# Weighted rows stored slot by slot within a feature, and half-chunks of gathers left out, in the two GAT layers of a four-layer graph network

## The reference

```python
def gat_conv(h, src, dst, fc_w, attn_l, attn_r, bias, heads, out_feats):
    feat = (h @ fc_w.T).reshape(n, heads, out_feats)
    el = jnp.sum(feat * attn_l, axis=-1)
    er = jnp.sum(feat * attn_r, axis=-1)
    e = jax.nn.leaky_relu(el[src] + er[dst], 0.2)
    m = jax.ops.segment_max(e, dst, num_segments=n)
    ex = jnp.exp(e - m[dst])
    ssum = jax.ops.segment_sum(ex, dst, num_segments=n)
    a = ex / ssum[dst]
    rst = jax.ops.segment_sum(feat[src] * a[..., None], dst, num_segments=n)
    return rst + bias.reshape(heads, out_feats)
...
h0 = gat_conv(inputs, src, dst, fc1_w, attn_l1, attn_r1, bias1, 8, 32)
h1 = jax.nn.relu(h0 + norm * (inputs @ wb0.T + bb0))
h2 = gat_conv(h1, src, dst, fc2_w, attn_l2, attn_r2, bias2, 1, 256)
```

## Time and profile before

| what | value |
|---|---|
| median of 3 runs | 7953.76 us (7950.26 to 7963.52) |
| the profiled execution, its own time | 7953.61 us |
| its span in the trace | 7951.9 us |
| busy in the span | DVE 70%, POOL 67%, PE 42%, ACT 16% |
| gat1, roughly from 3260 to 4540 us | 1280 us |
| gat2, roughly from 4540 to 5830 us | 1290 us |

### The profile page before, as it was taken

One profiled execution on the slowest core, in us unless ns is written; L12 is line 12 of the kernel. 1 busy time (PEld: TensorE's weight loads), 2 busy tenths in 40 slices (PEclk: granted clock), 3 DMA queues, 4 the chain that ended last, 5 costly groups with the idle time before them and its releaser, 6 DMA issues. The chain is left out here.

```text
span 7951.9 us, 73782 instructions
## 1 busy us (share of the span) xinstructions
PE 3326.4 (42%) x15180; PEld 2659.3 (33%) x15181; DVE 5588.3 (70%) x11215; ACT 1251.3 (16%) x2729; POOL 5351.3 (67%) x4985
## 2 busy tenths in 40 slices
PE   3445454444677767212222200000025555555556
PEld 3233333334666666101111100000024444444434
DVE  7578888884333343688888677777766778777756
ACT  3101111111011111000000000001022332222312
POOL 0667676665777777577777677777757777776521
PEclk7766767667878888555555555555557787777767
DMA  2346656552332332233333233333322333333210
GB/s 84 88 129 169 165 154 166 161 142 76 85 88 84 86 88 76 64 92 97 88 98 93 65 79 98 90 89 98 86 82 84 112 105 104 107 103 96 76 35 13
DMA packets 489232, 773.99 MB, mean 97 GB/s; under 512 B 298796, under 2 KB 319767, under 8 KB 485436
## 3 DMA queue, kind: packets, MB, share of 16 engines
q0 software_dynamic: 265920, 667.09, 30.5%
q10 hardware_dynamic: 20536, 77.34, 2.6%
q1 hardware_dynamic: 202688, 28.69, 2.3%
HBM read 823.08 MB, written 46.52 MB: 109 GB/s over the span
## 5 line engine op out<-in xcount | busy, mean ns | idle before, releaser
L1021 POOL DMA_INDIRECT gat_rows<-scratch_gat,gat_index x1856 | 1858.4, 1001 | 583.4 <-issue 542.4
L1934 POOL DMA_INDIRECT m_rows<-scratch_gat,m_index x928 | 1217.9, 1312 | 508.8 <-issue 272.9
L1021 POOL DMA_INDIRECT conv_rows<-scratch_kv,conv_index x928 | 929.8, 1002 | 424.4 <-issue 252.1
L1467 POOL DMA_INDIRECT rel_rows<-scratch_x,rel_index x928 | 1016.0, 1095 | 295.4 <-issue 279.4
L1317 PE MATMUL conv_ps<-conv_work,k_ident 128*128 128x256 f32 x1856 | 679.2, 545 | 751.1 <-DVE conv_work L1100 679.5
L724 PE MATMUL gat_ps<-k_ident,gat_cur 128*128 128x128 f32 x100 | 34.5, 448 | 2127.7 <-DVEq L1184 1201.7
L1317 PEld LDWEIGHTS conv_ps<-conv_work,k_ident 128*128 128x128 f32 x1856 | 520.5, 288 | 910.2 <-issue 721.1
L724 PEld LDWEIGHTS gat_ps<-k_ident,gat_cur 128*128 128x128 f32 x100 | 14.5, 203 | 2163.3 <-DVEq L1184 1220.1
L1732 PE MATMUL rel_ps<-rel_factor,rel_rows 128*128 128x128 f32 x3712 | 600.3, 338 | 270.6 <-DMA rel_rows<-scratch_x,rel_index 270.3
L1732 PEld LDWEIGHTS rel_ps<-rel_factor,rel_rows 128*128 128x128 f32 x3712 | 582.5, 251 | 282.7 <-DMA rel_rows<-scratch_x,rel_index 175.1
L1112 DVE TENSOR_REDUCE gat_red<-gat_work 128x256 f32<-128x2048 f32 x182 | 652.4, 3584 | 0.0
(11 more groups left out here) (488 smaller groups left out, 7569.5 us busy)
## 6 DMA issues: line engine op xcount, KB each, us to landing
m_bc<-scratch_bc ACTq DMA_DIRECT2D x25, 2048.0 KB, 8.6
gat_rows<-scratch_gat,gat_index POOLq DMA_INDIRECT x1856
conv_rows<-scratch_kv,conv_index POOLq DMA_INDIRECT x928
rel_rows<-scratch_x,rel_index POOLq DMA_INDIRECT x928
m_rows<-scratch_gat,m_index POOLq DMA_INDIRECT x928
scratch_runs<-e_runs_sb ACTq DMA_DIRECT2D x1, 6453.1 KB
scratch_runs<-e_runs_sb SPq DMA_DIRECT2D x1, 6437.5 KB
scratch_kv<-p_row ACTq DMA_DIRECT2D x25, 256.0 KB, 2.5
```

The source lines that it names most:

```text
L1021: pool.indirect_dma_start(out=rows[b][:, s, :], out_offset=None, in_=table, in_offset=bass.IndirectOffsetOnAxis(ap=index[b][:, s:s + 1], a ...
L1467: pool.indirect_dma_start(out=rows[b][:, g, :], out_offset=None, in_=dr["x1"], in_offset=bass.IndirectOffsetOnAxis(ap=index[b][:, g:g + 1] ...
L1934: pool.indirect_dma_start(out=rows[b][:, s, :], out_offset=None, in_=dr["gat3"], in_offset=bass.IndirectOffsetOnAxis(ap=index[b][:, s:s + ...
```

## The change

Two things are done in `gat1` and `gat2`.

1. `work` becomes `[P, F, S]`. The multiply now writes the features of one slot 8 numbers (32 bytes) apart, and the reduction reads the 8 slots of a feature next to each other.
2. Where the second half of a tile's last chunk is empty for all its nodes (largest degree at most 8 x chunks - 4, and at least 3 chunks), POOL issues only the first four gathers of that chunk. Two new rows of `sched` tell this for each tile, with the sums over the tiles before it, since the semaphore `gathered[b]` no longer grows by 128 for every use. VectorE and SP work out their wait values from these sums. VectorE computes on all 8 slots as before; the four that were not fetched hold rows of an earlier use and have weight 0 by the mask.

In `attend_and_scan` the same helpers are called with `halves=False`, which gives the wait values and the gathers of before.

```diff
@@ fetch_nodes
+            st.add(v.tensor_scalar(free[:], per[:, 0, :], float(S), float(-S // 2), ALU.mult, ALU.add))
+            st.add(v.tensor_scalar(half[:, 0, :], per[:, 0, :], 3.0, None, ALU.is_ge))
+            st.do(v.tensor_tensor(half[:, 1, :], per[:, 1, :], per[:, 2, :], ALU.subtract))
+            st.do(v.tensor_tensor(free[:], free[:], first[:], ALU.is_ge))
...
+            for k in range(2):
+                st.do(v.tensor_tensor_scan(wholes[:, k, :], whole[:, k, :], zero[:], 0.0, ALU.add, ALU.add))
+                st.do(v.tensor_tensor(wholes[:, k, :], wholes[:, k, :], whole[:, k, :], ALU.subtract))
...
+            st.add(v.tensor_copy(kp["sched"][:, WHOLE, 0:T], half[:, 0, :]))
+            st.do(v.scalar_tensor_tensor(half[:, 0, :], tile_no[:], -64.0, half[:, 0, :], ALU.mult, ALU.add))
+            st.do(v.tensor_scalar(kp["sched"][:, LATER_WHOLE, 0:T], half[:, 0, :], 64.0, None, ALU.add))
@@
+HALF = 16 * (S // 2)
+class Halves:
+    def read_halves(self, read, row, t):
+        word = read(row, t, 0, (CHUNKS_MAX // 2 << 6) + 63)
+        self.last_whole, self.whole_tails, self.whole_pairs = word & 1, (word >> 1) & 31, word >> 6
+    def whole_now(self, j, b):
+        if b == TAIL_BUF:
+            return self.last_whole
+        return (self.pairs > j + 1) | self.last_whole | self.tail
+    def landed_before(self, j, b):
+        if not self.halves or b not in (1, TAIL_BUF, SECOND):
+            return self.uses(j, b) * (2 * HALF)
+        return self.uses(j, b) * HALF + (self.whole_pairs + j if b == 1 else self.whole_tails + self.firsts(b)) * HALF
+    def landed(self, j, b):
+        if not self.halves or b not in (1, TAIL_BUF, SECOND):
+            return (self.uses(j, b) + 1) * (2 * HALF)
+        now = 1 if b == SECOND else self.whole_now(j, b)
+        return self.landed_before(j, b) + HALF + now * HALF
+def gather_slots(pool, w, j, b, one):
+    for s in range(S // 2):
+        one(s)
+    if not w.halves or b not in (1, TAIL_BUF):
+        for s in range(S // 2, S):
+            one(s)
+        return
+    with pool.If(w.whole_now(j, b) > 0):
+        for s in range(S // 2, S):
+            one(s)
@@ edge_layer
-        work = [sb(f"work{b}", [P, S, F]) for b in range(3)] if pe_sums else [sb("work", [P, S, F])] * 3
+        halved = not pe_sums
+        work = [sb(f"work{b}", [P, S, F]) for b in range(3)] if pe_sums else [sb("work", [P, F, S])] * 3
@@ load_record
-                sp.wait_ge(gathered[b], 16 + u * 16 * S)
+                sp.wait_ge(gathered[b], 16 + w.landed_before(a, b))
@@ gather
-                for s in range(S):
+                def one(s):
                     pool.indirect_dma_start(
...
+                gather_slots(pool, w, a, b, one)
@@ logits
-                v.wait_ge(gathered[b], 16 + (u + 1) * 16 * S)
+                v.wait_ge(gathered[b], 16 + w.landed(a, b))
@@ weigh
-                v.tensor_tensor(work[b][:].rearrange(per_head, h=H),
-                                rows[b][:, :, values:values + F].rearrange(per_head, h=H),
+                weighted = work[b][:].rearrange(per_head if pe_sums else "p (h d) s -> p s h d", h=H)
+                v.tensor_tensor(weighted, rows[b][:, :, values:values + F].rearrange(per_head, h=H),
                                 over_dims(prob[:, 0:S, :], D), ALU.mult).then_inc(released[b], 1)
...
-                    slots = work[b][:].rearrange("p s f -> p f s")
+                    slots = work[b][:]
```

More of the change, by code:

```diff
@@ L392, in fetch_nodes @@
         more, cum_more, all_records = sb("f_more", [1, T]), sb("f_cummore", [1, T]), sb("f_allrecords", [1, T])
+        free, half = sb("f_free", [1, T]), sb("f_half", [1, 3, T])
+        whole, wholes = sb("f_whole", [1, 2, T]), sb("f_wholes", [1, 2, T])
         has_more, long_tiles = sb("f_hasmore", [1, T]), sb("f_longtiles", [1, 1])
@@ L797 @@
 HANDED = {"conv": "x1", "gat1": "gat2", "gat2": "gat3"}
-CHUNKS, RECORDS, USES, COUNT, CODE, TAILS, LATER, LATER_CODE, MORE, MORE_AT, WORD = range(11)
+CHUNKS, RECORDS, USES, COUNT, CODE, TAILS, LATER, LATER_CODE, MORE, MORE_AT, WORD, WHOLE, LATER_WHOLE = range(13)
 TAIL_BITS = 5
@@ L809, with __init__ @@
 TAIL_BUF = 2
-class Visit:
-    def __init__(self, eng, kp, t):
+FIRST_BUF, SECOND = 3, 4
+HALF = 16 * (S // 2)
+assert T < 32
+class Halves:
[25 more added lines that the diff above has]
+            one(s)
+class Visit(Halves):
+    def __init__(self, eng, kp, t, halves=False):
         def read(row, at, least, most):
@@ L828, in __init__, with firsts @@
         self.chunks_end = self.chunks + count
+        self.halves = halves
+        if halves:
+            self.read_halves(read, WHOLE, t)
+    def firsts(self, b):
+        return 0
     def uses(self, j, b):
@@ L835, in chunk, with __init__, read @@
         return self.chunks + j * 2 + (0 if b == TAIL_BUF else b)
[L838 to L848, removed]
+class Stay(Halves):
+    def __init__(self, eng, kp, t, halves=False):
+        def read(row, at, least, most):
+            return eng.value_load(kp["sched"][0:1, row, bass.ds(at, 1)], min_val=least, max_val=most)
+        code = read(LATER_CODE, t, 0, (CHUNKS_MAX // 2 << TAIL_BITS) + T)
+        later = read(LATER, t, 0, E // S + 2)
         self.t, self.later = t, code >> TAIL_BITS
@@ L853, in __init__, with firsts @@
         self.chunks = self.later + self.records + t
+        self.halves = halves
+        if halves:
+            self.read_halves(read, LATER_WHOLE, t)
+    def firsts(self, b):
+        return self.t + (1 if b == TAIL_BUF else 0)
     def uses(self, j, b):
@@ L886, in stay, with visit @@
         chunk(w, w.pairs, TAIL_BUF)
-def visit(eng, kp, t, chunk, in_first=None):
-    w = Visit(eng, kp, t)
+def visit(eng, kp, t, chunk, in_first=None, halves=False):
+    w = Visit(eng, kp, t, halves)
     if in_first is None:
@@ L1046, in _ @@
             for t in range(2):
-                visit(pool, kp, t, gather)
+                visit(pool, kp, t, gather, halves=halved)
             with tile_loop(nc, pool, 2, T) as t:
-                visit(pool, kp, t, gather, first_pair(t - 2))
+                visit(pool, kp, t, gather, first_pair(t - 2), halves=halved)
             if handed:
@@ L1193, in tile @@
             def tile(t, first):
-                w = Visit(v, kp, t)
+                w = Visit(v, kp, t, halves=halved)
                 st = new_steps(v, steps)
@@ L1937, in gather @@
                         bounds_check=limit, oob_is_err=False).then_inc(gathered[b], 16)
+                gather_slots(pool, w, j, b, one)
             with tile_loop(nc, pool, 0, T) as t:
```

19 lines of the change are left out of this document (14 added, 5 removed).

## The result

The changed kernel takes 8001.58 us (median of 4 runs, 7998.44 to 8008.73), the kernel before 7952.64 beside it: a ratio of 1.0064 with an interval of 1.0053 to 1.0076. The forecast had the wrong sign. The time lies in the range, and the rival "the write costs more than the read did" had named 8004. But that rival's price, 4.2 us a multiply, was not met; the larger part of what went wrong lies elsewhere. In the experiments further down, 2 of 25 runs of the kernel before were slow (8040 and 8254 us); its median hardly feels them, but the intervals of the ratios are wider for them.

The account below looks back on a forecast made before the run. The prediction took POOL's gathers as the bound, VectorE close behind. From 7953.6 us, -72 for the skip, +16 for register work and +4 for setup, multiply and reduction cancelling, gave 7902 us; range 7812 to 8040.

Parts of the forecast that it names:

- the write costs more than the read did: Rival, chance 0.22: VectorE's multiply at 4.2 us, +0.6 us a chunk, gat1 slower skip or no skip; 8004 us.
- What bounds the kernel: In gat1 and gat2: POOL is full, VectorE some 1.4 us a five-chunk tile behind in gat1, some 4 in gat2.
- The skip: POOL's gathers in 13 tiles per layer: 104 fewer, 135 us of POOL, of which VectorE's slack lets 72 us count.
- The set-up: 20 more operations in `fetch_nodes`, whose end VectorE sets: +4 us.
- The reduction: VectorE's sum over slots: 2.29 us in place of 3584 ns, -1.30 us per chunk, 232 times.
- The multiply: VectorE's write 8 numbers apart: 2288 ns today, between 2.29 and 4.91 us after, taken as +1.30 us.
- I take that the write pays what L1112's read paid: VectorE's multiply: the stepped write costs +1.30 us, like the reduction's stepped read of 2048 numbers.
- the two then cancel, the chunk stays as it is: VectorE's chunk: multiply +1.30 us, reduction -1.30 us, so its length is unchanged and the 72 us stand.
- ScalarE's ratio: Upper end for VectorE's multiply: ScalarE's stepped write costs 2.2 times as much, giving 4.91 us.
- The register work: VectorE's wait values and one more load per tile: 0.15 us a chunk, 0.2 a tile; +16 us (0 to 30).
- it counts where VectorE binds: VectorE's register operations: charged only in the 13 skipping tiles, 36 chunks of buffers 1 and 2 a layer.

Follow-up runs that it names:

- e3: e2 with the register work moved from VectorE and SP to ScalarE, which raises a semaphore per chunk; 7884.51 us, ratio 0.9899 to the kernel before.
- e2: The changed kernel with the old `work` layout, keeping the skip and its bookkeeping; 7966.70 us, ratio 1.0013 to the kernel before.
- e4: The changed kernel, new layout included, with its register work moved to ScalarE as in e3; 7918.87 us, ratio 0.9953 to the kernel before.
- e5: e3 with the reduction replaced by three additions of halves; on slower chips, three sets: ratios 0.9850, 0.9874 and 0.9854 to the kernel before.
- e8: e2 with the reduction replaced by three additions of halves; on slower chips, two sets: 9020.86 and 9019.13 us, ratios 0.9891 and 0.9882 to the kernel before.
- step9: The kernel before with a work tile of 9 numbers per feature, 8 used; 9222.48 us in one run on a slower chip.
- step24: The kernel before with a work tile of 24 numbers per feature, 8 used; slower chips: 9160.93 us in one run, repeat 9213.25, ratio 1.0084.

## Why the prediction was wrong

- **What bounds the kernel**: right. POOL first, VectorE 1.4 us a tile behind in `gat1`. VectorE's own 52.2 us for five chunks came out as 51.8 in e3 and, with what the change adds, 52.2 + 2.2 + 0.6 = 55.0 after, where tiles that skip took 54.8 to 54.9 and the others 55.1 to 55.3.
- **The skip**: right. 1752 gathers, POOL's pitch unbroken at 0.306 us of issue, no price for the branches. The term of -72 us with the set-up's +4 gives -68; e3, which has these and hardly anything else, shows -64.
- **The set-up**: +4 forecast. POOL's L633, the first operation behind it, starts at 276.36 us instead of 272.60: +3.8.
- **The reduction**: right, 2.28 us for 2.29.
- **The multiply: mis-sized.** The step "I take that the write pays what L1112's read paid" gave 3.58 us and let write and read cancel. It is 3.84, and the chunk pays 0.13 us net. The step "the two then cancel, the chunk stays as it is" also overlooked that the multiply releases the buffer and the reduction does not: even at equal prices the release would come 1.3 us later. Where the skip was to use all the slack, the layout is worth 30 to 34 us (e2 to the change, e3 to e4). I had a row at this very step of 8, and put it to the rival because the row of 2048 numbers seemed nearer. Its price was worked out wrongly, too: the 1.89 ns come from comparing with the one-head form, whose 8 numbers lie side by side, so that the step differs as well as the count. By the earlier trace rows, 8 numbers side by side at 1.04 ns leave 161 - 8 = 153 ns beside, and (267 - 153) / 64 is 1.79 ns at a step of 8. That is the 1.80 which the write shows, and would have given 3.81 us for the multiply. The step, not the size of the operation, was the right guide. (ScalarE's ratio, too, gives 4.85 us and not 4.91 by its own rows; nothing hangs on it.)
- **The register work: the step that failed.** I took 0.15 us a chunk and 0.2 a tile, with 0.3 as the upper bound, and counted it in the 13 skipping tiles alone. Measured, from gap to gap of a tile of five chunks, are +0.93, -0.20, +0.58, +0.25 and +0.66 us, together 2.2. And it counts in all tiles of `gat1` but the first: 2.2 us are more than the slack of 1.4, so VectorE becomes the bound even where nothing is skipped. In `gat2`, with 4 us of slack, it counts in the skipping tiles only. The forecast of +16 us, at most 30, stands against 78 to 82 (the change less e4, e2 less e3). The error had two halves. The bound came from a gap that already hid part of such work, the 0.56 us between 0.31 and 0.87, instead of from the gap that hid none, the 0.23 behind `gat_hid`, where every register instruction shows in full. And "it counts where VectorE binds" was asked of the kernel before and not of the changed one.

Put back into the sum, 7953.6 - 72 + 4 + 34 + 80 is 8000, against 8001.6 measured; since the 34 and the 80 were read from differences between these same kernels, this tests the first two terms and no more. That the rival of the dearer write gave 8004 is in part chance: its mechanism, VectorE taking over as the bound in `gat1`, skip or no skip, is what happened, but at 3.84 us a multiply it would have been slower by little or nothing (it was said to turn the sign at 3.9): e4, with that multiply and little register work on VectorE, is 29 us faster than the kernel before. The register work, listed as a small term, supplied the rest. That e5 and e8 are faster than the kernel before, with the same skip, is measured; that the tiles of `gat1` behind the first wait for VectorE alone after the change is read from the timeline.

## What to carry to other kernels

Where two engines pass buffers to each other within a few per cent, a saving on the one counts only up to the other's slack, and whatever bookkeeping the saving needs must be charged to the other engine in every tile. Look where a computed wait value falls: behind an operation that its successor followed at once, each register instruction is idle time of the whole engine, and an engine that is 16% busy can compute it and hand it on by a semaphore. Ask also on which side of a release a cost falls: what moves from behind it to ahead of it is paid by the engine that waits. Instead of trading a stepped read for a stepped write, look for a form with neither: three additions of halves replaced the reduction and saved 1.25 us of the chunk's operations.

## What the hardware did that I had not expected

- The price of VectorE's write of 2048 float32 numbers is no single surcharge for a step: 1.04 ns a number side by side (2288 ns), 1.80 at a step of 8 (3837), 1.78 at 9 (3799), 2.50 at 24 (5272). Reading runs of 8 of which half begin at odd places costs nothing more: 2278 ns in step9, 2286 in step24.
- Eight register instructions ahead of an operation, with no data to wait for, lengthened the gap from 0.23 to 1.16 us; one more scalar load with the work on its number at a tile's start took 0.66.
- A semaphore handed on by ScalarE cost VectorE nothing to be seen in `gat1`: in e3 the gaps are 0.23, 0.81, 0.32, 0.73 and 1.44 us, against 0.23, 0.87, 0.31, 0.87 and 1.45.
